# One state of a pair moves from TensorE's sum to VectorE's in a selective scan

## The reference

```python
x = x + _L0_xattn_ref(ctx, _layernorm(x), wq, wk, wv)
gate = sigmoid(h @ W_gate.T + b_gate)            # h = layernorm(x)
x_proj, delta_proj = split(h @ W_in.T + b_in, 2)
delta = relu(delta_proj)
# per channel (512) and state n (16), over the 32 tokens:
#   s_n = s_n * exp(A_n * delta_t) + (x_t * delta_t) * B_n
#   y_t = sum over n of s_n * C_n      (C is one row, the same for all)
x = x + (gate * (y + x_proj * D_vec)) @ W_out.T + b_out
```

## Time and profile before

| | us |
|---|---|
| median of 3 executions | 1806.5 (1802.24, 1806.5, 1808.88) |
| profiled execution, own time | 1806.77 |
| its span | 1805.0 |
| busy in the span: TensorE / VectorE / ScalarE / GpSimd | 1650.3 / 1504.4 / 1493.5 / 1201.2 |
| L640, TensorE, 128 records | 592 ns median of one |
| L1042, VectorE, 96 | 743 to 745 ns median of one |

### The profile page before, as it was taken

One profiled execution on the slowest core, in us unless ns is written; L12 is line 12 of the kernel. 1 busy time (PEld: TensorE's weight loads), 2 busy tenths in 40 slices (PEclk: granted clock), 3 DMA queues, 4 the chain that ended last, 5 costly groups with the idle time before them and its releaser, 6 DMA issues. The chain is left out here.

```text
span 1805.0 us, 41933 instructions
## 1 busy us (share of the span) xinstructions
PE 1650.3 (91%) x14031; PEld 1129.4 (63%) x14031; DVE 1504.4 (83%) x2771; ACT 1493.5 (83%) x3463; POOL 1201.2 (67%) x1430
## 2 busy tenths in 40 slices
PE   7999999999999999999999843679999999999974
PEld 4666566666666666675665512557777777777752
DVE  5449989989989989989989898547788888888853
ACT  4579999989989989989989876137788888888864
POOL 3547767676766767768667654068788887878852
PEclk9999999999999999999999875799999999999976
DMA  9413122221322223122130130000000000000000
GB/s 259 142 54 117 53 100 83 79 104 54 106 77 71 88 77 106 54 85 98 57 114 30 56 105 0 18 10 14 13 17 15 15 15 15 15 15 15 12 8 12
DMA packets 54226, 107.12 MB, mean 59 GB/s; under 512 B 8400, under 2 KB 30928, under 8 KB 49232
## 3 DMA queue, kind: packets, MB, share of 16 engines
q1 hardware_dynamic: 54096, 105.51, 17.8%
HBM read 96.97 MB, written 8.52 MB: 58 GB/s over the span
## 5 line engine op out<-in xcount | busy, mean ns | idle before, releaser
L763 ACT ACTIVATE abuf<-delta,cols 128x496 f32<-128x496 f32 x512 | 331.8, 707 | 5.5 <-DVE yac L1025 3.1
L933 POOL TENSOR_TENSOR yac<-yac,gP 128x1024 f32<-128x1024 f32 x128 | 302.8, 2365 | 40.9 <-ACT gP L772 39.6
L1025 DVE TENSOR_TENSOR_SCAN gP<-abuf,ps_s 128x512 f32<-128x512 f32 x256 | 296.3, 1200 | 0.4 <-POOL yac L933 0.4
L581 PE MATMUL ps_kv<-w_k,cT 128*128 128x256 f32 x1024 | 255.2, 392 | 0.0
L593 PE MATMUL ps_kv<-kcube,cx 128*128 128x256 f32 x1024 | 248.6, 386 | 0.6 <-ACT kcube L803 0.5
L593 PEld LDWEIGHTS ps_kv<-kcube,cx 128*128 128x128 f32 x1024 | 190.2, 190 | 58.8 <-issue 27.9
L923 POOL TENSOR_TENSOR kcube<-kcube,ksq 128x512 f32<-128x512 f32 x128 | 166.1, 1298 | 81.1 <-ACT ksq L785 81.1
L653 PE MATMUL ps_kv<-hT,w_pT 128*128 128x512 f32 x384 | 189.4, 617 | 32.9 <-ACT delta L848 25.8
L581 PEld LDWEIGHTS ps_kv<-w_k,cT 128*128 128x128 f32 x1024 | 184.0, 189 | 48.9 <-issue 29.0
L772 ACT ACTIVATE gP<-gP,cols 128x512 f32<-128x512 f32 x256 | 170.3, 718 | 0.0
L913 POOL TENSOR_TENSOR rat<-s,roots 128x8 f32<-128x8 f32 x64 | 105.9, 1655 | 93.3 <-ACT junk L792 93.3
(11 more groups left out here) (326 smaller groups left out, 4076.6 us busy)
## 6 DMA issues: line engine op xcount, KB each, us to landing
cT<-in_h_ctxT SPq DMA_DIRECT2D x32, 1028.0 KB, 7.4
cx<-in_ctx SPq DMA_DIRECT2D x32, 1024.0 KB, 5.4
xT<-in_h_xT SPq DMA_DIRECT2D x8, 512.0 KB, 3.6
xcur<-in_x SPq DMA_DIRECT2D x32, 128.0 KB, 2.0
left_n<-in_ctx SPq DMA_DIRECT2D x128, 32.0 KB, 1.9
x_mid<-xb SPq DMA_DIRECT2D x16, 256.0 KB, 2.4
x_c<-x_mid SPq DMA_DIRECT2D x32, 128.0 KB, 2.0
out<-y SPq DMA_DIRECT2D x32, 128.0 KB, 1.7
```

The source lines that it names most:

```text
L581: last = pe.matmul(bank[:, j * D:(j + 1) * D], cT[G % 2][:, b, dc, j * P:(j + 1) * P], w_k[:, dc, :], start=False, stop=(dc == DC - 1), sk ...
L763: act.activation(abuf[q % 2][:, i, :].rearrange("p (b t) -> p b t", t=T)[:, :, 1:T], delta[J % 2][:, :].rearrange("p (b t) -> p b t", t=T) ...
L933: pool.tensor_tensor(yac[:, :, :], yac[:, :, :], pool_home(q)[:, :, :], ALU.add).then_inc(S["pacc_done"], 1)
L1025: dve.tensor_tensor_scan(dst[:, i, :], abuf[q % 2][:, i, :], ps_u[:, :], 0.0, ALU.mult, ALU.add).then_inc(S["scan_done"], 1)
```

## The change

TensorE sums only state 0 of pair 0 (one diagonal matmul instead of two, which starts and closes the bank alone). A new VectorE instruction, `dve_weigh_first`, adds weight times state 1 of pair 0 onto `ps_y`, right after the scan of pair 6 and before `dve_weigh` of that pair. The semaphore `y_state` counts one more per block, the scan of the next block's pair 0 waits for it as well, and the diagonal matrices made once are four instead of eight.

```diff
-NACC = 2 * len(BY_DVE) - 1
+NACC = 2 * len(BY_DVE)
...
-    diag = sb("diag", [P, CB, 2 * NPE, P])
+    diag = sb("diag", [P, CB, P])
...
         if k == 0 and J == 0:
-            pe.wait_ge(v["s_diag"], CB * 2 * NPE)
-        pe.wait_ge(S["scan_done"], NST * J + 2 * q + 2)
-        if k == 0 and J:
+            pe.wait_ge(v["s_diag"], CB)
+        pe.wait_ge(S["scan_done"], NST * J + 2 * q + 1)
+        if J:
             pe.wait_ge(S["y_read"], J)
-        for i in range(2):
-            last = pe.matmul(ps_y[:, :], diag[:, J % CB, 2 * k + i, :], pe_home(J, q)[:, i, :], start=(k == 0 and i == 0),
-                             stop=(k == NPE - 1 and i == 1))
-        last.then_inc(S["y_full"], 1)
+        pe.matmul(ps_y[:, :], diag[:, J % CB, :], pe_home(J, q)[:, 0, :], start=True, stop=True).then_inc(S["y_full"], 1)
...
             if J and k == 0:
-                dve.wait_ge(S["y_state"], NACC * (J - 1) + 2)
+                dve.wait_ge(S["y_state"], NACC * (J - 1) + 3)
...
             if J:
                 dve.wait_ge(S["y_full"], J)
+                dve.wait_ge(S["y_state"], NACC * (J - 1) + 1)
...
+    def dve_weigh_first(dve, Z):
+
+        n = 2 * BY_PE[0] + 1
+        dve.wait_ge(S["y_full"], Z + 1)
+        dve.wait_ge(S["scan_done"], NST * Z + n + 1)
+        dve.scalar_tensor_tensor(out=ps_y[:, :], in0=pe_home(Z, BY_PE[0])[:, 1, :], scalar=w_st[:, Z % CB, n:n + 1], in1=ps_y[:, :],
+                                 op0=ALU.mult, op1=ALU.add).then_inc(S["y_state"], 1)
...
         dve.wait_ge(S["scan_done"], NST * Z + n + 1)
-        if k == 0 and i == 0:
-            dve.wait_ge(S["y_full"], NPE * (Z + 1))
-        else:
-            dve.wait_ge(S["y_state"], NACC * Z + 2 * k + i)
+        dve.wait_ge(S["y_state"], NACC * Z + 2 * k + i + 1)
...
             dve_scan(dve, Z, 6)
+            dve_weigh_first(dve, Z)
             dve_weigh(dve, Z, 0, 0)
...
+        n = 2 * BY_PE[0]
         for cb in range(CB):
-            for i in range(2 * NPE):
-                n = 2 * BY_PE[i // 2] + i % 2
-                dve.tensor_scalar(diag[:, cb, i, :], ident[:, :], w_st[:, cb, n:n + 1], None, ALU.mult).then_inc(v["s_diag"], 1)
+            dve.tensor_scalar(diag[:, cb, :], ident[:, :], w_st[:, cb, n:n + 1], None, ALU.mult).then_inc(v["s_diag"], 1)
```

## The result

| | before | after |
|---|---|---|
| median, us (executions beside each other) | 1806.6 (9) | 1801.5 (9), from 1798.9 to 1804.9 |
| ratio, 95% interval | | 0.9972 [0.9961, 0.9983] |
| profiled execution, own time / span | 1806.77 / 1805.0 | 1801.93 / 1800.1 |
| steps a, b, c, d | 30.53, 30.99, 34.36, 32.76 | 30.82, 31.38, 33.74, 32.53 |
| period | 128.64 | 128.47 |

The change is worth -5 us, 0.3%, less than the 0.5% that was called no change, and inside the range; the forecast was 1806.4 and the range 1800 to 1814. A step is measured here from one start of VectorE's `mx` reduction (L1071 before, L1074 after) to the next, averaged over steps 10 to 29. These lengths repeat within 0.02 us in a second execution of either kernel.

A forecast was written before the change was run, and what follows sets the result against it. VectorE was taken to bound steps a and b, TensorE c and d. The terms 0.3 - 0.6 + 0.6 - 0.9 + 0.5 gave -0.1 us: 1806.77 - 0.1 = 1806.7, less 0.3 to the median, 1806.4; range 1800 to 1814.

The forecast's parts named there:

- steps a, b, c, d: The first loop's repeating four steps: a and b set by VectorE, c and d, with the output projection, by TensorE.
- TensorE gives up 0.86, VectorE takes 0.84: Each of 32 first-loop steps: one of two equal matmuls goes, 0.86 us; the new chained VectorE instruction costs 0.84.
- a pays 0.30 because L1131's 0.54 is given back: Step a: VectorE arrives 0.84 later, finds GpSimd's L938 done, and L1131 loses its 0.54 stall: net +0.30.
- The first rival: L1131's 0.54 is not given back, so a pays 0.84: +6.1 in all, 1812.6 us; chance 0.18.
- b pays 0.34: Step b: TensorE, held at L712 for VectorE's copy, is 0.6 later, less the 0.3 of a; b about 31.3.
- c gains 0.86, 0.8 with what is left of b: Step c: TensorE saves 0.86, is not held at L712 (reserve 2.0), and reaches L606 0.2 earlier than now.
- third rival: ScalarE's results hold TensorE in c, its 0.86 is lost, a and b pay 0.84 each: +13.5, 1820 us; chance 0.13.
- d pays 0.1: 0.84 less the short waits of 0.75: Step d: VectorE starts 0.2 early, pays 0.84, and its short waits of 0.75 go: -0.1 against the present.
- A period is 128.5, -0.1: Four first-loop steps together: 0.1 us less than 128.61, so -0.6 over the six periods of steps 6 to 29.
- Steps 31 to 36: +0.3 - 0.9 + 0.5 = -0.1: End of the first loop: step 31 +0.3, step 32 -0.9 behind the shortened L640, step 33 +0.5, 34 to 36 nothing.
- six periods, steps 5 and 30 to 36: The whole sum, first loop only: +0.3, -0.6, +0.6, -0.9 and +0.5, together -0.1 us.
- second rival: TensorE is not held at L712 in b, so savings of b and c both count: -5 to -7, 1800 to 1802; chance 0.13.

The follow-up runs named there:

- pe_only: Kernel before with the matmul of state 1 of pair 0 left out and nothing in its place: 1792.9 us, ratio 0.9928.
- pad_dve: Kernel before with 91 empty instructions on VectorE, which left nothing in the compiled program: 1804.7 us, ratio 0.9999.
- pad_pe: Kernel after with 128 empty instructions on TensorE, which left nothing in the compiled program: 1800.7 us, ratio 0.9979 to before.
- dve_only: Kernel after with both TensorE matmuls kept, so state 1 of pair 0 counts twice: 1810.8 us, ratio 1.0026 to before.
- pad_dve2: Kernel before with waits that hold nothing, 91 instructions more in VectorE's program (3101): 1805.0 us, ratio 0.9991.
- pad_pe2: Kernel after with waits that hold nothing, 128 instructions more in TensorE's program (17215): 1803.5 us, ratio 0.9983 to before.
- before_again: Kernel before once more, no edit: 1806.25 us, ratio 1.0004.
- cd_only: Kernel after, but VectorE takes state 1 only where the sum falls in steps c and d, TensorE elsewhere: 1808.0 us, ratio 1.0018 to before.
- cd_pad: cd_only with waits that hold nothing, 44 instructions more on VectorE (3101) and 64 on TensorE (17215): 1797.7 us, ratio 0.9957 to before.

## Why the prediction was right, and where it was not

**The verdict was right and the first loop's sum was of the right size, but nearly all of the 5 us came from something that it didn't consider. That this stayed inside the range is luck: the place of the code alone is worth up to 10 us here, and the range reached down by 6.**

- *TensorE gives up 0.86, VectorE takes 0.84.* Measured 0.86 and 0.83.
- *a pays 0.30 because L1131's 0.54 is given back.* Right: +0.29, the update takes 0.35, and without GpSimd's L938 it takes 0.344 to 0.347 in every step. The first rival (0.84 in a) is refuted.
- *b pays 0.34.* Measured +0.39. TensorE was forecast to be held once, for pT, with a gap of 1.2; it is held twice, 0.69 for ScalarE's delta and 0.33 for pT. I had looked for its next dependence on VectorE only.
- *c gains 0.86, 0.8 with what is left of b.* Measured -0.62. The step asked whether TensorE is held at L712 and found 2.0 in reserve, but the first thing behind the shortened product is the projection, which needs ScalarE's hT, with 0.77 in reserve. pe_only shows the same -0.62 with VectorE untouched. This is a small piece of the third rival (ScalarE takes TensorE's place in c), at 0.23 a step instead of the 0.86 it was priced at.
- *d pays 0.1: 0.84 less the short waits of 0.75.* Measured -0.23. All three waits went, but each gave back more than its idle time. Against the step's start VectorE is 0.87 late at the copy pT, 0.52 late behind the first wait (0.26 of idle), 0.13 behind the second (0.30), and 0.16 early behind the third (0.19): 1.03 and not 0.75. An instruction that follows a wait doesn't overlap the end of the one before it, and that overlap is some 0.08 each time.
- *A period is 128.5, -0.1.* Measured 128.47, -0.18: six of them are -1.1 where the sum had -0.6. That it comes so near is in part luck: c gained 0.2 less than forecast and d came out 0.3 shorter. With steps 5 and 30, +0.27 and +0.28 where the sum had +0.3 each, steps 5 to 30 are 0.6 shorter; the sum had 0.0.
- *Steps 31 to 36: +0.3 - 0.9 + 0.5 = -0.1.* Not settled. The first two pairs of traces have -1.1 and -0.8, the third (pad_dve, pad_pe) +2.9. One and the same program takes 142.0 or 144.4 us there, so pe_only's 1.9 less and dve_only's 0.2 more can't be read either. Over 1003 to 1118 us TensorE's granted clock is 0.74 in before and 0.76 in pad_dve: it goes down and up there, and not in the same places.
- *The second loop: not in the sum.* It has no edit, so I priced it at nothing. Its 5.0 us less, in the mean of three traces each, are the step that failed: "six periods, steps 5 and 30 to 36" was taken for the whole. What the runs showed in its place is the place of the code: 91 instructions more in VectorE's program shorten an iteration from 17.69 to 17.61 us (pad_dve2), and 128 fewer in TensorE's take away the pause behind the start of the last iteration and move the other from the ninth iteration to the fifth (pad_pe2 has both back). pad_dve2 and pad_pe2 are before and after with programs of the same lengths, and between them lie 1.5 us (1805.0 and 1803.5), less than their intervals can tell apart. So beyond the 0.6 us of steps 5 to 30 no gain of the change itself is shown.

One point would have misled a reader of the profile alone: in after, TensorE's clock is low at 66 to 70 us (granted 0.61), and steps 2 and 3 are together 1.6 us longer than in before. pad_dve, whose compiled program is that of before, has such a stretch too (0.78 over 66 to 72 us), and its step 2 is 1.6 longer; before_again has none. So it comes without the change. But all traces of after have it and only one of three of before, so that the change makes it more frequent isn't ruled out.

The second rival (TensorE not held, 1800 to 1802) names the measured time, but not its reason: TensorE is held in b.

## What to carry to other kernels

A move of work between engines in step pays only in the steps that the giving engine sets, so do it in those steps alone: taking state 1 from TensorE in c and d only gave 4.2 us more in the first loop than taking it everywhere. Before crediting a saving, look up the next operand of each instruction behind it on that engine, from every other engine: the nearest cover was 0.77 on ScalarE, not 2.0 on VectorE. And an edit that changes a program's length moves everything behind it in the instruction stream: compare versions at equal program lengths, or pad both, before giving a difference of 0.3% (here up to 10 us, cd_only against cd_pad) to the edit itself.

## What the runs showed of the hardware that I had not expected

- Place alone moved a kernel's time by 10.3 us (1808.0 to 1797.7) through pauses of TensorE of 1.2 to 1.8 us beside block loads of its instructions, and its clock at 1.2 GHz behind most of them.
- 91 places in VectorE's program change a later loop's iteration from 17.69 to 17.61 us. The first thing that moves within an iteration is a register operation of VectorE, from 2.41 to 2.31 us behind the iteration's start; it is the next instruction of VectorE's sequencer behind the iteration's only branch, which stands at 2.12 in both. What it is about the place stays open.
- The same compiled program differs from one execution to the next in where TensorE's clock falls, and its steps 31 to 36 took 142.0 us in one execution and 144.4 in another. Whether the clock is the cause isn't shown. Two pairs of traces agreed on a gain of 1.4 to 1.6 us in the first loop, and the third pair took it back.
- A VectorE instruction held by GpSimd shows as a longer duration and not as a wait (0.88 instead of 0.34). The Trainium skill's "SBUF — State Buffer", section "Who interferes with whom", has the rule (a Vector instruction with two SBUF inputs against a GpSimd instruction that reads SBUF); the removal of GpSimd's instruction bears it out.
